# Eight unused columns more in the plan tensor of a fused LoRA feed-forward kernel

## What is computed

```
gate = x @ W_gate.T + 0.5 * (x @ A_gate[i].T) @ B_gate[i].T        # 512 -> 1376
up   = x @ W_up.T   + 0.5 * (x @ A_up[i].T)   @ B_up[i].T          # 512 -> 1376
act  = silu(gate) * up
down = act @ W_down.T + 0.5 * (act @ A_down[i].T) @ B_down[i].T    # 1376 -> 512
m    = max(abs(down), over the row, at least 1e-5)
out  = x + ((down / m) @ Q.T) * (m * scale) + bias                  # Q: weights of 2 bits
```

## Time and profile before

| | |
|---|---|
| time, median of 3 runs | 947.43 us (946.28 to 947.5) |
| the profiled execution's own time | 943.36 us |
| its span, first to last instruction | 941.4 us |
| mean granted TensorE clock | 0.993 of full speed |
| TensorE matmul busy | 905.0 us, 96% of the span |
| TensorE weight load busy | 718.0 us, 76% |
| VectorE, ScalarE, GpSimd busy | 350.2, 254.5 and 80.1 us |
| DMA | 45.38 MB, 48 GB/s over the span |

### The profile page before, as it was taken

The page is one execution under the profiler, slowest core; times in us unless marked ns, Lnnn a source line. Parts: engine busy times, 40 slices in busy tenths (PEclk is TensorE's granted clock), DMA queues, the critical chain, the costliest instruction groups (busy, mean ns, idle before and its releaser), DMA issues.

```text
span 941.4 us, 13785 instructions
## 1 busy us (share of the span) xinstructions
PE 905.0 (96%) x3954; PEld 718.0 (76%) x3954; DVE 350.2 (37%) x762; ACT 254.5 (27%) x448; POOL 80.1 (9%) x110
## 2 busy tenths in 40 slices
PE   3899899999999999999999999999999999999994
PEld 3677677777777777777777777777777777777773
DVE  3543355322542234422352224432254223532233
ACT  2432334111422124211242113411242212421111
POOL 0010001200120001201002001010012000200100
PEclk9999999999999999999999999999999999999998
DMA  4442322111211111110111101101121111100011
GB/s 122 124 137 72 103 72 55 46 46 27 56 49 39 28 30 56 47 40 25 33 55 33 43 23 52 53 18 42 28 56 49 39 29 28 34 11 22 22 34 48
DMA packets 45445, 45.38 MB, mean 48 GB/s; under 512 B 13168, under 2 KB 31984, under 8 KB 45392
## 3 DMA queue, kind: packets, MB, share of 16 engines
q1 hardware_dynamic: 43312, 41.98, 16.4%
q10 hardware_dynamic: 2080, 2.88, 0.9%
HBM read 36.44 MB, written 8.39 MB: 48 GB/s over the span
## 4 chain that ended last, share of the span: by engine, by line
PE 91%; DVE 2%; SPq 2%; DMA 2%; ACT 1%; issue 1%; DVEq 0%; ACTq 0%
PE pp_up L1745 25%; PE pp_gate L1745 23%; PE pp_down L1822 23%; PE ps_misc L1849 6%; PE ps_td L1811 4%; PE ps_misc L1745 2%; PE pp_down L1832 2%; PE pp_up L1792 2%; PE pp_gate L1792 2%; PE ps_misc L1840 1%; DMA rows<-w_gu 1%; SPq L336 1%; SPq L350 0%; DMA b_raw<-places 0%; DMA x_raw<-x_feat 0%
## 5 line engine op out<-in xcount | busy, mean ns | idle before, releaser
L1822 PE MATMUL pp_down<-wd,actp_split 128*128 128x512 f32 x960 | 236.9, 395 | 0.0
L1745 PE MATMUL pp_up<-xw,wgu 128*128 128x512 f32 x948 | 234.0, 396 | 0.0
L1745 PE MATMUL pp_gate<-xw,wgu 128*128 128x512 f32 x864 | 216.7, 400 | 3.1 <-ACT actp_full L967 3.0
L1822 PEld LDWEIGHTS pp_down<-wd,actp_split 128*128 128x128 f32 x960 | 180.1, 188 | 47.6
L1745 PEld LDWEIGHTS pp_up<-xw,wgu 128*128 128x128 f32 x948 | 178.4, 188 | 42.6
L1745 PEld LDWEIGHTS pp_gate<-xw,wgu 128*128 128x128 f32 x864 | 161.1, 189 | 40.8 <-issue 4.3
L1411 DVE TENSOR_TENSOR actp_full<-pp_up,actp_full 128x512 f32<-128x512 f32 (+1 forms) x87 | 60.1, 691 | 339.8 <-PE pp_up L1792 320.1
L967 ACT ACTIVATE actp_full<-pp_gate 128x512 f32<-128x512 f32 (+1 forms) x80 | 47.8, 597 | 291.5 <-PE pp_gate L1792 280.1
L983 ACT ACTIVATE actp_split<-actp_full 128x512 fp32r<-128x512 f32 x80 | 50.6, 632 | 176.6 <-DVE actp_full L1411 176.6
L1420 DVE TENSOR_TENSOR actp_split<-actp_full,actp_split 128x512 fp32r<-128x512 f32 x80 | 55.1, 689 | 16.7 <-ACT actp_split L983 16.7
L1849 PE MATMUL ps_misc<-wq,dtp_split 128*128 128x512 f32 x232 | 59.0, 395 | 0.6 <-DVE dtp_split L1443 0.6
(11 more groups left out here) (112 smaller groups left out, 624.4 us busy)
## 6 DMA issues: line engine op xcount, KB each, us to landing
x_raw<-x_feat SPq DMA_DIRECT2D x122, 64.0 KB, 1.7
rows<-w_gu SPq DMA_DIRECT2D x8, 512.0 KB, 3.9
rows<-x_tok SPq DMA_DIRECT2D x64, 64.0 KB, 1.8
more_rows<-x_tok SPq DMA_DIRECT2D x64, 64.0 KB, 1.8
out<-rows SPq DMA_DIRECT2D x60, 64.0 KB, 1.6
out<-more_rows SPq DMA_DIRECT2D x60, 64.0 KB, 1.6
b_raw<-b_rows SPq DMA_DIRECT2D x32, 92.0 KB, 2.8
b_raw<-b_rows SPq DMA_DIRECT2D x32, 80.0 KB, 2.5
```

Of the source, the lines that this page charges most:

```text
L1745: return nc.tensor.matmul(ps_out[0:m, a:b], w, xw[:, part, k, a:b], start=start, stop=stop)
L1822: last = nc.tensor.matmul(pp_down[:, s, :], actp_split[0:w, ap, f % 2, s * P:(s + 1) * P], wd[0:w, wp, f, :], start=(f == 1 and n == 0), s ...
```

## The change

The `plan` tensor gets 8 columns behind its last one, which nothing reads or writes. It grows from 292 to 324 bytes in each partition, that is from 320 to 352 with the rounding. Every buffer that is declared behind it, from `xw` (and its overlay `xs`) on, moves up by 32 bytes: those at 96 come to lie at 0. The columns in use keep their places, and no instruction is added, taken away or moved. The other changed line is an empty one, which shifts the line numbers behind it by one.

```diff
@@ -119,7 +119,8 @@
         rinv = sb("rinv", [P, WIDE_SUBS])
         ascale = sb("ascale", [P, WIDE_SUBS])
 
-        plan = sb("plan", [P, BATCH // 2 + WIDE_TILES + 1], I32)
+
+        plan = sb("plan", [P, BATCH // 2 + WIDE_TILES + 1 + 8], I32)
         plan_run = plan[0:1, BATCH // 2:BATCH // 2 + WIDE_TILES]
         plan_flag = plan[0:1, BATCH // 2 + WIDE_TILES:BATCH // 2 + WIDE_TILES + 1]
```

## The result

The changed kernel takes 932.96 us (median of 4 runs, 931.64 to 934.85) where the kernel before takes 946.86 beside it (4 runs, 946.14 to 947.5). The ratio is 0.9869, 95% interval 0.9852 to 0.9886. The forecast of 947.4 us, with a range from 944.5 to 949.5, was wrong: the gain of 13.9 us is seven times what this measurement can tell from nothing.

The account below looks back on a forecast made before the run. The prediction took TensorE's matmul-to-matmul distance as the bound. Its terms, 0 for TensorE, -0.1 to 0 us for VectorE and -0.05 to +0.05 for the last stores, left the median at 947.4 us, range 944.5 to 949.5.

Parts of the forecast that it names:

- What bounds the kernel: From 138 to 910 us, 82% of the span, only the distance from one matmul to the next sets the time.
- TensorE, 512 columns: Projection and down matmuls: 234, 233 and 232 ns for three operand placements, so no cost of a start at 96 shows.
- TensorE, both at 0: 256-column warm-up, 120.0 against 117.5 ns: both operands at 0 isn't faster; bounds 9.4 us slower, 6.4 us faster.
- TensorE's term of the sum: All TensorE matmuls together: taken as 0 us.
- Rival A: TensorE matmuls read faster with both operands at 0: at most -6.4 us, 941.0 us; chance 0.03.
- Rival B: TensorE matmuls slower because weight and moving reads in one phase collide: +9.4 us, 956.8 us; chance 0.03.
- The lines of 16 bytes: SBUF reads: 96 and 128 are both multiples of 16, so a contiguous read meets equally many lines; effect 0.
- The other engines: VectorE -0.1 to 0 us; ScalarE 0 and hidden; GpSimd 9 ns for each of 16, hidden; last DMA stores within 0.05 us.
- VectorE's seven ns: 128x512 SBUF passes: 684 ns at 0 against 691 at 96, so at most 0.1 us where exposed.
- The DMA rule that spoke against the change: more_rows transfers start further past a 256-byte multiple: an estimated 1.5% more, some hundredths of a us for the last stores.
- The remark on 96 and 32: Buffers that move are 96 past a multiple of 128, not 32, and still arrive at a multiple; no size.
- Rival C: Whole kernel: nothing moves but medians differ by chance, about 944 or 950 us; chance 0.07, half to each side.

Follow-up runs that it names:

- e10: Changed kernel with the L1793 matmuls filled with zero rows from 96 to 128; 929.08 us, ratio 0.9821.
- e12: e10 with the stationary operands of L1812 (64 or 32 columns) also widened to 128 columns; 925.55 us, ratio 0.9793.
- e2: Kernel before with xw left at 96 and everything behind it moved to 0; 939.73 us, ratio 0.9947.
- e3: Kernel before with the weights and all other buffers ahead of plan moved to 96 too, so every matmul operand is at 96; 930.53 us, ratio 0.9850.
- e8: Kernel before with 72 columns of padding ahead of xw, for a distance of 256 bytes; no time given here, but described as having the whole gain.
- e11: The changed kernel again, unaltered, measured beside e10; 930.49 us, ratio 0.9849.

## Why the prediction was wrong

**What bounds the kernel** was right: the distance between matmuls sets 82% of the span, and 11.2 of the 11.8 us of span came from six steady tiles.

**TensorE, 512 columns** was the step that failed. Its three rows of starts were read right, at 234, 233 and 232 ns, but the conclusion from them was not. L1745 and L1822 both have one operand at 0 and one at 96, so they have the same kind of distance and can't differ by theory R. The third, "both at 96", was the one control of 512 columns at distance 0. It came from L1792 and L1811, which have 96 rows or 32 to 64 columns, and that keeps them slow even where all around them is at distance 0: 230 to 233 ns in the changed kernel, and 227 once e10 and e12 give them the full shape. (That in the kernel before their neighbours at other distances held them up as well isn't ruled out.) The control differed from the case in a second thing, and that thing hid the effect.

**TensorE, both at 0**, the second failure. The lower bound let an address cost no more than the 1.7 ns of a matmul that don't grow with its columns, worked out from matmuls of 256 and 512 columns at distances of 32 either way. No run shows such a limit: at 512 columns distance 0 took off 6.7 ns each at best and 3.7 to 5.2 in the mean of the two big lines. And the 256-column warm-up, 120.0 against 117.5 ns, was used as if it could stand for 512 columns. The changed kernel's own first tile says it can't: its 256-column matmuls on `xw`, now at distance 0, take 119.5 ns (mean of 21 at full clock) where those of before took 117.8 (29). Seven more runs with these at distance 0 have 119.0 to 119.8, and e2, at -32, has 118.3. So at 256 columns distance 0 is a loss of some 1.7 ns, while at 512 it gains up to 6.7. The 2.5 ns that the prediction set down to the resolution were in good part real, but held for 256 columns only. Nine of them in order of time, to be set beside the earlier trace rows:

```profile
19.02 1.24 PE L1746 MATMUL pp_gate<-xw,wgu_first 128*128 128x256 f32 x9
```

1.24 us less the last one's 0.28 is 0.96 for 8, 120.0 ns: what the warm-up showed. TensorE's term of the sum was 0 with bounds of -6.4 and +9.4 us; the whole change measured -13.9, twice the lower bound, and six tiles alone have -11.2 of it.

**Rival A** had the right sign and the right remark ("a penalty that comes whenever either operand is at 96 would look just like" the rows), but the wrong cause (e3 has no operand at 0 and is as fast), less than half the price, and 3 chances in 100. **Rival B** named what counts, how the places of the two operands lie to each other, but with the wrong sign: equal places are what is fast at 512 columns. That it comes from two reads that meet is argued there and isn't shown by the runs. The 189 ns of the whole warm-up, which B took as a sign of something besides place, are 213 ns each up to 16.3 us and about 120 behind it, on the same addresses.

**The lines of 16 bytes.** The rule from the Trainium skill's "SBUF — State Buffer", "Specifications (TRN2)", gave 0 for each operand by itself, since all places are multiples of 16. It says nothing of how two operands lie to each other. The prediction's sum by it was 0 and the measurement is -13.9 us, and the measurement decides: shifts of 32 bytes changed the time, and what counts is the distance within 256 bytes. My sentence that no page has a unit of 64 or 128 bytes made an argument of the pages' silence.

**The other engines** came out as forecast. VectorE's seven ns between 691 and 684 were not the address, though: at 0 it is 693. The DMA rule that spoke against the change ("DMA: Bandwidth & Descriptors", "How a descriptor splits into AXI transactions") has no row that would show it: `out<-more_rows` takes 1.6 us before and after. **The remark on 96 and 32** was right and pointed at nothing, since the place past a multiple of 128 doesn't matter by itself, only the difference to the weights. **Rival C** played no part: the medians of the kernel before were 946.86 us beside the changed one and 944.96 to 945.43 beside the experiments, so a time differs by up to 1.9 us between calls, and only the ratios within a call are used.

## What to carry to other kernels

Where matmuls of 512 fp32r columns, each with a weight load of its own, follow each other without a gap at full clock, place the moving operand so that its start and that of the stationary one differ by a multiple of 256 bytes. For 256 columns this case shows no gain, and none at the lower clock. Check by the start-to-start distance of a group and not by the mean in a row: for `pp_up<-xw,wgu` that mean was 396 ns before and 391 after, and neither is what a matmul costs. Keep narrow matmuls (few rows, few columns) out of the row, or fill them up with zeros if they cost no time of their own. And a control that shows no effect is worth only as much as its likeness to the case: look at what else differs.

## What the runs showed of the hardware

- A 512-column fp32r matmul of full shape at full granted clock (2.4 GHz) came every 226.7 ns at distance 0 in an unbroken row, and in the mean every 230 to 234 ns at the other distances. At the lower level (1.2 GHz, 0.50 in the rows) it came every 427 ns at distances of -32, 0, +96 and 128 alike.
- A 256-column one came every 213 ns at the lower level, and every 117 to 120 at full clock (117.8 at -32, 119.5 at 0). Both figures of the lower level are one column per cycle of 1.2 GHz (256 / 1.2 = 213.3, 512 / 1.2 = 426.7) with nothing left over. At 2.4 GHz 512 columns would be 213.3 ns by the same count, and take 13.4 more at best. What limits them there isn't shown.
- The warm-ups of both kernels came every 213 ns as well, up to 16.3 us before and to the end after, though the profile gives the granted clock there as 1.00: by the distances it was at the lower level.
- The steps repeat. The distances by position in a group of `pp_up` agree to 1 ns between the changed kernel, e8 and e11: after a break 237, 233, 230, then 227. It looks like two reads that have to fall in step again; that it is so is argued, not shown.
- Open is which of the two neighbouring weight loads is the partner of a moving operand, and what happens at distances that aren't multiples of 32 bytes.
